# Order of TensorE's work in a slot of a cross-attention kernel: the scores before or after the weighted sums

## The reference

```python
a = _layer_norm(audio_kv, ln_gamma, ln_beta)
Q = (hidden_states @ Wq.T)...; K = (a @ Wk.T)...; V = (a @ Wv.T)...
scores = jnp.einsum('bhtd,bhsd->bhts', Q, K) * scale      # mask, then
attn = jax.nn.softmax(scores, axis=-1)
out = jnp.einsum('bhts,bhsd->bhtd', attn, V)
out = out @ Wo.T
return hidden_states + jnp.tanh(gate) * out
```

## Time and profile before

| | |
|---|---|
| median of 3 runs | 1026.55 us (1025.28 to 1027.88) |
| the profiled execution | 1022.71 us, its span 1020.5 us |
| granted TensorE clock, mean of the span | 0.987 |
| TensorE busy, matmul | 989.4 us, 97% |
| TensorE busy, weight load | 831.9 us, 82% |
| VectorE, ScalarE, GpSimd busy | 73%, 65%, 71% |
| DMA | 102.26 MB, 100 GB/s in the mean |

### The profile page before, as it was taken

How to read it: one execution, slowest core, us unless ns; L and a number is a source line. 1 busy time by engine, 2 the same in 40 slices (tenths; PEclk the granted TensorE clock), 3 DMA queues, 4 the chain that set the end, 5 groups by cost and what they waited for, 6 DMA issues and landing times.

```text
span 1020.5 us, 32130 instructions
## 1 busy us (share of the span) xinstructions
PE 989.4 (97%) x11665; PEld 831.9 (82%) x11665; DVE 748.4 (73%) x1414; ACT 661.7 (65%) x1364; POOL 719.8 (71%) x977
## 2 busy tenths in 40 slices
PE   9997999999999999999999999999999999999975
PEld 8896887888888888878888888888888888888863
DVE  6640388887877777787777787778887787877773
ACT  3313577766766766777666776667776676776662
POOL 1447878787777777787777787777878777775221
PEclk9999999999999999999999999999999999999997
DMA  9653433333334344433433443444333334331111
GB/s 298 195 160 68 124 93 83 88 100 105 81 104 106 101 109 107 108 88 88 103 85 96 110 105 102 109 107 110 85 95 102 90 89 112 82 81 30 31 36 41
DMA packets 83252, 102.26 MB, mean 100 GB/s; under 512 B 29024, under 2 KB 65888, under 8 KB 83200
## 3 DMA queue, kind: packets, MB, share of 16 engines
q10 hardware_dynamic: 24652, 56.60, 20.5%
q1 hardware_dynamic: 58548, 44.94, 17.1%
HBM read 91.34 MB, written 10.19 MB: 99 GB/s over the span
## 4 chain that ended last, share of the span: by engine, by line
PE 48%; DMA 26%; DVE 18%; issue 3%; POOL 1%; ACT 1%; SPq 1%; DVEq 0%; POOLq 0%; ACTq 0%
PE bank L766 33%; DMA row_max<-rmax 12%; DMA x<-row_max 10%; DVE rmax L714 7%; PE sbank L860 5%; PE bank L876 5%; DVE shared_f L724 4%; DVE bank L704 2%; DVE stats L673 2%; PE bank L782 2%; DVE top L701 1%; PE bank L885 1%; PE bank L881 1%; DMA row_stats<-row_stat 1%; PE sbank L782 1%
## 5 line engine op out<-in xcount | busy, mean ns | idle before, releaser
L766 PE MATMUL bank<-shared_r,w_k 128*128 128x376 f32 x1536 | 300.0, 344 | 5.8 <-ACT shared_f L622 5.7
L766 PE MATMUL bank<-w_v,shared_r 128*125 128x512 f32 x1152 | 284.8, 396 | 0.0
L766 PEld LDWEIGHTS bank<-shared_r,w_k 128*128 128x128 f32 x1536 | 259.6, 189 | 27.7 <-issue 21.1
L600 ACT ACTIVATE shared_f<-shared_f 125x448 f32<-125x448 f32 x384 | 201.4, 586 | 92.3 <-DVE shared_f L724 92.0
L766 PEld LDWEIGHTS bank<-w_v,shared_r 128*125 128x125 f32 x1152 | 213.3, 186 | 45.3
L714 DVE TRANSPOSE_TENSOR_REDUCE rmax<-shared_f 128x14 f32<-128x448 f32 x384 | 216.4, 614 | 36.5 <-ACT shared_f L569 36.4
L569 ACT ACTIVATE shared_f<-sbank,mask_b 125x448 f32<-125x448 f32 x384 | 215.7, 636 | 25.7 <-PE sbank L860 25.6
L724 DVE TENSOR_TENSOR shared_f<-shared_f,bank 125x448 f32<-125x448 f32 x384 | 215.4, 616 | 4.5
L452 POOL TENSOR_TENSOR shared_f<-shared_f 125x448 f32<-125x448 f32 x128 | 150.3, 1174 | 93.7 <-ACT shared_f L600 91.4
L413 POOL TENSOR_TENSOR cn<-cn,stat_bc 128x375 f32<-128x375 f32 x128 | 117.7, 952 | 91.3 <-DMA cn<-in_ctxT 76.8
L701 DVE TENSOR_REDUCE top<-x 128x14 f32<-128x168 f32 x128 | 55.9, 437 | 138.9 <-DMA x<-row_max 138.7
(11 more groups left out here) (65 smaller groups left out, 901.6 us busy)
## 6 DMA issues: line engine op xcount, KB each, us to landing
cn<-in_ctxT ACTq DMA_DIRECT2D x30, 750.0 KB, 6.0
rows<-in_ctx ACTq DMA_DIRECT2D x28, 720.0 KB
stat_bc<-row_stats ACTq DMA_DIRECT2D x29, 375.0 KB, 4.3
x<-row_max SPq DMA_DIRECT2D x128, 84.0 KB
xy<-in_x SPq DMA_DIRECT2D x32, 224.0 KB, 3.9
out<-xy SPq DMA_DIRECT2D x32, 224.0 KB
shared_f<-in_xT SPq DMA_DIRECT2D x7, 896.0 KB, 9.2
rows<-in_ctx SPq DMA_DIRECT2D x4, 720.0 KB
```

What stands on the lines that cost most here:

```text
L600: act.activation(prob[0:SP_, (r - 3) % NB, j, :], prob[0:SP_, (r - 3) % NB, j, :], ACT.Exp, scale=SCALE).then_inc(exp_done, 1)
L766: last = pe.matmul(dst, l, m, start=(start and k == 0), stop=(stop and k == len(pairs) - 1))
```

## The change

In TensorE's slot the scores move behind the weighted sums and denominators. K, V and the output keep their places, and no other engine's order changes.

```diff
                 if is_slot(i, r, -1):
                     transpose_mask()
-                if live(i, LOOP, r, SLOTS):
-                    scores(i, r)
                 if live(i, LOOP, r - 3, SLOTS):
                     if is_slot(i, r, 3):
                         pe.wait_ge(mask_out, 1)
                     weighted_sum(i, r)
+                if live(i, LOOP, r, SLOTS):
+                    scores(i, r)
```

## The result

| | before | after |
|---|---|---|
| median of 16 runs | 1024.47 us (1021.14 to 1031.58) | 1031.15 us (1026.84 to 1036.63) |
| the profiled execution, span | 1022.71, 1020.5 us | 1029.05, 1026.8 us |
| granted clock, mean of the span | 0.987 | 0.986 |

The ratio is 1.0069, with a 95% interval of 1.0048 to 1.009. The kernel became slower, as forecast, but by 7 us in the medians where the forecast had some 20.

What follows compares the result with a forecast made beforehand. TensorE, 97% busy at 7.00 us a slot, was taken as the bound. 19.5 (path 2) + 1.5 (head) + 1.1 (end) - 1.9 (old waits) = 20.2 us on 1022.7 gave 1042.9, or 1047 us as median; range 1030 to 1063.

Steps and rivals of the forecast that it cites:

- part 1: TensorE's own stream: only seams between matmul groups change, each set by what stands before; cost 0, bounds -7 and +26 us.
- part 2: Every path from a slot's scores through other engines to a later slot's weighted sums has 1.95 us less room.
- Path 2: Maxima read behind the `cn` load: loop of 14.59 to 14.91 us against TensorE's 14.00; 0.75 us per batch, 19.5 us.
- Path 3 alone binds: Rival: the maxima read doesn't wait for `cn`, GpSimd's loop costs 0.2 us per batch, about 5 us; 1032 us; chance 0.16.
- Path 3: GpSimd centres `cn`, then makes its sum: loop of 14.0 to 14.3 us, parallel to path 2 and shorter, adds nothing.
- Start and end: 1.5 us for the head (about 1.2 in slot 6, a little for slots 4 and 8), 1.1 us at the end.
- The seam's rival: With waits absent, a denominators-to-scores seam of 0.11 rather than 0.17 us gains 7 us; 1020 us; chance 0.06.
- No new wait lasts: Rival: `cn` also lands sooner, every loop fits into 14.00 us; only head, tail and old waits, +0.7 us; 1027; chance 0.10.
- the footing: The median of the runs was put 3.8 us above the profiled execution, taking the forecast from 1042.9 to 1047 us.

Runs made afterwards that it cites:

- experiment 2: The changed kernel with the old order (scores first) in slots 126 and 127 only; median 1027.16 us, ratio 1.0061 to the kernel before.
- experiment 1: The changed kernel with the old order (scores first) in slots below 12 only; median 1029.24 us, ratio 1.0078 to the kernel before.
- experiment 10: The changed kernel with the rows load issued in slot u = 0 of the next batch instead of u = 2; ratio 1.0072 to the kernel before.
- experiment 5: The changed kernel with the rows load of slots with u = 2 issued behind its slot's first exponential; median 1028.65 us, ratio 1.0057.

## Why the prediction was off

**The seams (part 1) were right.** Weighted sums follow a projection by 0.37 to 0.38, the scores follow the denominators by 0.17, and K follows the scores by 0.11. A batch of 28.02 us without waits is 0.02 over that of before.

**The room of 1.95 us (part 2) was right**, and so was the arithmetic of a loop. In experiment 2 `top` came at 9.69; with 3.84 and 1.10 that gives 14.63, and 14.63 is what the rows show. In experiment 1 it gives 14.70 against 14.64.

**Path 2 failed at one step: it carried the 9.65 and 9.97 us "from the scores with u = 2 to `top` with u = 0" over to the new order, because "the loads are tied to the scores, through the L569 ahead of them on ScalarE".** I took an interval that was equal in two batches for a coupling. The loads also stand behind L600, which waits for VectorE's subtraction, and behind L585, which waits for the weighted sums. In slots 19 to 103 of before, L263 is issued 0.50 us after the (modelled) end of the denominators' matmuls in 6 batches, those of slots 18 and 98 among them, and 0.48 us after the end of the last subtraction (L724) in the other 16; L250 follows 0.6 us later. The batch of slot 46:

```profile
422.93 0.74 PEld L860 LDWEIGHTS sbank<-shared_f 32*125 32x125 f32 x24 [0.38 <-issue]
...
425.18 1.68 DVE L724 TENSOR_TENSOR shared_f<-shared_f,bank 125x448 f32<-125x448 f32 x3
...
427.94 0.41 ACTq L250 DMA_DIRECT2D cn<-in_ctxT  x1
```

There `cn` goes out 5.01 us after the scores. Over the 22 batches the interval is 3.12 to 5.01 us, and `top` comes at 9.49 to 11.85, 10.54 in the mean and not 9.81. The two batches read were not typical: by the sum's own working 10.54 would have made 1.48 us per batch and not 0.75, so that the forecast is not farther off is luck. The wait of the earlier trace rows belongs to the longest, slot 46 with 11.85.

With the change the weighted sums come 1.10 us ahead of the scores rather than 0.85 behind them, and the subtraction ends before the scores do. The last thing awaited is then L569's scores, L263 follows their end by 0.82 us in all 22 batches, and the interval became 2.35. The maxima's write moved as well: from 0.88 to 2.69 us before the scores with u = 2 to 3.6 before them. In the profile of after, the read then passes `cn`, `top` comes at 6.54 in most batches, and path 2 costs nothing from slot 10 on. The rival "Path 3 alone binds" came near this, but by the write getting ahead of the rows load. It did not: in slot 18 it stands 1.57 us behind that load (1.22 before), and both go out earlier against the scores. Where the read stays behind, `top` comes at 9.33 in the mean (experiment 1), and the price is 0.27 us per batch and not the 0.75 of the sum, some 7 us instead of 19.5.

**Path 3 "is next in line" was right as an order, and the 5 us of its rival was near, in part by luck.** The rival asked for an unchanged `cn` issue, and with that it would have cost more: in experiment 10, where the read is ahead as well, the four batches with `cn` issued 2.96 to 3.18 us after the scores (slots 18, 26, 34 and 46) take 14.31 to 14.81 us for two slots, 0.64 over 14.01 in the mean. That would be an estimated 17 us in 26 batches. With the load at 2.35, GpSimd just fits, and only nine waits of 5.1 us in all are left. The two errors, an issue put too late and a price put too low, went against each other.

**Start and end were undersized in the profiled execution.** Slot 6 was near (1.50 against "about 1.2"), but slots 3 and 4 add 0.91 and 1.03 us, where I had "a little", and slots 8 and 12 have 0.47 and 0.96, against 1.13 and 0.35 in before. In all the start is 2.70 and not 1.5. It is no fixed cost, though: experiment 2, with the same start, had 0.65 (187.52 against 186.87). The end is 2.18, not 1.1; with the old order in the last two slots it is 0.38 (experiment 2), so the new order there is its cause. Which steps add up to it is open.

**The seam's rival** fell with the seam's 0.17. **"No new wait lasts"** had the right loop, nearly, but not the right start and end: with those of the profile (1.2 and 1.1 us more) it would have said 1029.5 rather than 1027.

The changed kernel's median of 1031.15 lies at the low end of the range, near the 1032 of the rival "Path 3 alone binds" and 16 us below the forecast. Of that, 2 us are the footing: the three runs shown had 1026.55, sixteen had 1024.47. How many of its executions have which order is not known, since one was profiled. Nor is it settled what chooses between the two orders. The change's start seems to favour the early read (experiment 1 lost it), but experiment 2 shows both with one program, so that is not shown.

## What to carry to other kernels

An interval measured in one order of the program is a sum of waits, and equal values in two batches don't say on whom it hangs. Before an edit moves something, list all instructions ahead of the one that counts in its queue, with the semaphore of each, and move every one of them as the edit does. When two loops are within a few tenths of the bound, expect several outcomes from one program, and try a remedy in each of them: the same edit took the waits out of the loop here in one order and cost 1% in the other. A profile shows one execution: what it shows of the start, or of the order of two transfers, can be otherwise in the next.

## What the runs showed of the hardware

**Two orders of transfers, each of which lasts.** Experiment 2 had the read behind `cn` in the sixteen batches from slot 18 to slot 78 and ahead of it in all from slot 82 on, without any difference in the instructions.

**Small transfers beside large ones.** A read of 84 KB issued 0.15 us ahead of a 720 KB load on another queue was used 7.31 us later (experiment 10); issued with no load just ahead of it, the same kind took 3.48 us. A write of 21 KB issued 0.43 us ahead of a 720 KB load had landed after 2.79 us, one issued 0.14 us ahead after 6.27 (experiment 5), and one issued 1.22 us behind after 6.62.

**When ScalarE's queue issues a load.** The first load of a group goes out a fixed time after the last of the events that the instructions ahead of it wait for, not when these instructions are done: 0.82 us after the scores' matmuls end, 0.50 after the denominators', 0.48 after VectorE's subtraction. This holds within 0.06 us in all 22 batches from slot 18 to slot 102 of before, of after and of experiment 10. In slot 19 of after it goes out at 232.49, while L569's second copy of three is running.

**Seams of the weight loads** go by what stands before and not by what follows: 0.37 to 0.38 us behind a projection with 512 columns, 0.17 behind the denominators, 0.11 behind the scores, with each of the two followers that the two kernels give them. Behind a K projection with 376 columns it was 0.24.
